# Cross attention in one fused perceiver layer: another order of the half-batches and another place for the projections

## The reference, cut to what matters

```python
x = x + cross_attention(layernorm(x), ctx_512)        # 16 batches x 64 queries, 1024 context rows of 128
x = x + self_attention(layernorm(x))
x = x + moe(layernorm(x))

# cross attention, per batch and head (16 heads):
kv_rope = kv_c * cos + rotate_half(kv_c) * sin
scores  = (q_r) @ (kv_rope @ W_kr).T                  # q_r from x, Wq, w_kc_q, W_qr
attn    = softmax(scores)                             # over the 1024 context rows
ctx_c   = attn @ kv_rope                              # 64 x 128 per head
ctx_lat = einsum('bhsd,hkd->bshk', ctx_c, w_kc_kv)
out     = ctx_lat.reshape(b, s, H * K) @ Wo.T         # 512 columns
```

## Time and profile before

| | us |
|---|---|
| median of 3 runs | 1516.76 (1516.18 to 1520.94) |
| the profiled execution | 1518.74 |
| its span, first to last instruction | 1516.9 |
| PE busy | 1361.9 (90%) |
| DVE busy | 809.9 (53%) |
| ACT busy | 734.6 (48%) |
| POOL busy | 573.7 (38%) |
| cross attention in the trace | about 155 to 802 |

### The profile page before, as it was taken

How to read it: one execution, slowest core, us unless ns; L and a number is a source line. 1 busy time by engine, 2 the same in 40 slices (tenths; PEclk the granted TensorE clock), 3 DMA queues, 4 the chain that set the end, 5 groups by cost and what they waited for, 6 DMA issues and landing times. The chain is left out here.

```text
span 1516.9 us, 22837 instructions
## 1 busy us (share of the span) xinstructions
PE 1361.9 (90%) x7136; PEld 1105.5 (73%) x7136; DVE 809.9 (53%) x1371; ACT 734.6 (48%) x1741; POOL 573.7 (38%) x346
## 2 busy tenths in 40 slices
PE   5998699999999999999985899999689979999992
PEld 4776578777777777777764688888578768777781
DVE  4434365656566666666544444444479863433235
ACT  2444465655555555555533577777521213333330
POOL 2122333333333332333103233333246466517985
PEclk9999799999999999999997999999699999999996
DMA  5786540323232323232315111112544246446667
GB/s 192 244 274 184 221 153 29 136 87 124 97 124 97 124 97 124 97 124 97 135 60 190 62 50 63 49 48 98 190 163 142 84 174 215 155 139 219 232 205 232
DMA packets 78984, 209.79 MB, mean 138 GB/s; under 512 B 5888, under 2 KB 39168, under 8 KB 72960
## 3 DMA queue, kind: packets, MB, share of 16 engines
q1 hardware_dynamic: 69472, 163.78, 30.4%
q0 software_dynamic: 7136, 38.80, 7.7%
q10 hardware_dynamic: 2304, 6.29, 1.1%
HBM read 154.59 MB, written 92.01 MB: 163 GB/s over the span
## 5 line engine op out<-in xcount | busy, mean ns | idle before, releaser
L660 DVE TENSOR_TENSOR probsT_lo<-psTr,probsT_hi 128x512 fp32r<-128x512 f32 x256 | 176.5, 690 | 199.9 <-ACT probsT_hi L610 199.5
L610 ACT CAST probsT_hi<-psTr 128x512 fp32r<-128x512 f32 x256 | 149.8, 586 | 211.7 <-PE psTr L750 211.0
L750 PE MATMUL psTr<-ident,probs 128*128 128x128 f32 x1024 | 152.5, 276 | 18.6 <-DVE probsT_lo L660 12.4
L750 PEld LDWEIGHTS psTr<-ident,probs 128*128 128x128 f32 x1024 | 122.3, 141 | 62.0 <-DVE probsT_lo L660 28.8
L527 POOL TENSOR_TENSOR ctxT_lo<-ctx_f,ctxT_hi 128x512 fp32r<-128x512 f32 x32 | 41.3, 1290 | 321.1 <-ACT ctxT_hi L579 321.1
L655 DVE TENSOR_REDUCE nmax<-psS 128x1 f32<-128x1024 f32 x128 | 155.4, 1214 | 11.5 <-PE psS L66 10.7
L572 ACT ACTIVATE probs<-psS,nmax 128x1024 f32<-128x1024 f32 x128 | 143.3, 1120 | 28.2 <-DVE nmax L655 28.2
L64 PE MATMUL bank<-w_slots,ao_first_hi 128*128 (+1 forms) x252 | 107.8, 428 | 15.3 <-DVE w_slots L1774 9.4
L64 PE MATMUL psV<-probsT_hi,kv_hi 128*128 128x512 f32 x256 | 117.3, 458 | 2.0
L64 PE MATMUL psS<-kT_hi,qe 128*128 128x512 f32 x256 | 113.1, 442 | 5.5 <-issue 4.7
L1480 POOL TENSOR_TENSOR w_slots<-w_ahead,w_slots 128x3072 fp32r<-128x3072 f32 x15 | 102.5, 6836 | 1.2
(11 more groups left out here) (268 smaller groups left out, 3328.8 us busy)
## 6 DMA issues: line engine op xcount, KB each, us to landing
w_ahead<-w_exp POOLq DMA_DIRECT2D x14, 1536.0 KB, 7.4
qe<-stage SPq DMA_DIRECT2D x16, 1024.0 KB, 6.7
qe<-qe SPq DMA_DIRECT2D x16, 1024.0 KB, 5.0
wraw<-w_pairs SPq DMA_DIRECT2D x8, 1792.0 KB, 11.3
early<-xs SPq DMA_DIRECT2D x47, 256.0 KB, 2.7
xs<-h_rows SPq DMA_DIRECT2D x47, 256.0 KB, 2.0
early<-ctx SPq DMA_DIRECT2D x16, 512.0 KB, 3.8
ao<-attn_out SPq DMA_DIRECT2D x32, 256.0 KB, 2.4
```

What stands on the lines that cost most here:

```text
L610: act.copy(PT[k % PTN].hi[:], psT[slot][:]).then_inc(turned_hi, 1)
L660: dve.tensor_tensor(out, psT[slot][:], f32(hi), ALU.subtract).then_inc(turned_free, 1)
L750: last = pe.transpose(psT[slot][:, q * P:(q + 1) * P], src(q), ident[:])
```

## The change

The four half-batches of a tile now go batch by batch inside a head half: c = 0, 1 are heads 0 to 7 of the first and second batch, c = 2, 3 heads 8 to 15. With that

- heads 0 to 3 of a tile are projected in its own c = 3, heads 4 to 7 in the next tile's c = 0, 8 to 11 in c = 1, 12 to 15 in c = 2 (`HEADS_AT`); in the last tile 4 to 15 come after c = 3. The semaphore counts halves of a projection;
- the K turns for the next tile's two batches are in c = 2 and c = 3 (steps 2 and 6), issued after the scores and ahead of the value product of the step; a second buffer holds the rotated context of the odd batch;
- the rope of the next tile's batches is on POOL's queue in c = 0 and 1; those of batches 0 and 1 are made in `build_queries`, after the second and the fourth pair's `split_low`, and the second context load is issued there;
- four K turns instead of two stand ahead of the first scores;
- residual, statistics and norm are at c = 2 (steps 4 to 7) and c = 3, k = 0; the turn of the normed rows at c = 3, k = 2;
- `kv_high` is at c = 0 and c = 3, k = 3; the probabilities' turned buffers are 3 instead of 4.

Cut to its core:

```diff
-def rope_kv(pool, keep, b):
+def rope_kv(pool, keep, b, j):
+
+    kv, kr, kt, tab = keep["kv_raw"], keep["kv_rope"][j], keep["kv_term"], keep["rope_tab"]
     ...
-        with sp.Fori(0, NP // 2 - 1) as i:
+        for p in range(2):
+            step(p, p, True)
+        sp.wait_ge(keep["rope_done"], 2)
+        sp.dma_start(keep["kv_raw"], t["ctx"][1]).then_inc(keep["kv_in"], 16)
+        with sp.Fori(1, NP // 2 - 1) as i:
     ...
-        with pool.Fori(0, NP // 2) as i:
+        pool.sem_inc(keep["rope_done"], 1)
+        for i in range(2):
             for j in range(2):
                 split_low(j, 2 * i + j)
-        pool.sem_inc(keep["rope_done"], 1)
-        pool.wait_ge(keep["tab_in"], 16)
-        rope_kv(pool, keep, 0)
+            if i == 0:
+                pool.wait_ge(keep["tab_in"], 16)
+            rope_kv(pool, keep, i, i)
+        with pool.Fori(2, NP // 2) as i:
+            for j in range(2):
+                split_low(j, 2 * i + j)
     ...
-PTN = 4
+PTN = 3
 K_STEPS, R_STEP = (2, 6), 4
+HEADS_AT = {0: {0: (4,), 1: (5,), 5: (6,), 7: (7,)}, 1: {0: (8,), 1: (9,), 5: (10,), 7: (11,)},
+            2: {0: (12,), 1: (13, 14), 3: (15,)}, 3: {5: (0,), 6: (1,), 7: (2, 3)}}
+TURN_H2_AT = (3, 2)
     ...
-        if hf == 0 and has_k and k in K_STEPS:
+        if c >= 2 and has_k and k in K_STEPS:
     ...
+        def iteration(i, first, last):
+            if not last:
+                fill(2 * i)
+                for j in range(2):
+                    load_kv(2 * i + 2 + j)
             for j in range(2):
-                load(2 * i + j, j, i, False)
-        for b in range(B, NBLK // NT):
-            sp.dma_start(t["xs_r"][b], t["zeros"]).then_inc(keep["fill_in"], 16)
+                if not last:
+                    sp.wait_ge(s_mm, RT * (HB * i + 3 + j))
+                    load_qe(2 * i + 2 + j, j)
+                if j == 0 and not first:
+                    sp.wait_ge(x1_made, i + 1)
+                    sp.dma_start(XT[:], x_d[i]).then_inc(xt_in, 16)
     ...
+                if c == 3 and not first:
+                    root(i - 1)
                 if not (first and c == 0):
                     ctx_low(n - 1, (c - 1) % HB)
-                if c == 1 and not first:
-                    root(i - 1)
-                if hf == 0 and has_k:
-                    kv_low(b + 1, 1 - j)
-                if hf == 1 and not last:
-                    pool.wait_ge(turned, place(b, 0, "K", 1, True)[0])
-                    pool.wait_ge(kv_lo, b + 2)
-                    rope_kv(pool, keep, b + 2)
-
-        iteration(0, True, False)
-        with pool.Fori(1, NT - 1) as i:
-            iteration(i, False, False)
-        iteration(NT - 1, False, True)
+                if c == 0:
+                    kv_low(2 * i + 1, 1)
+                if c == 3 and not last:
+                    kv_low(2 * i + 2, 0)
+                if c < 2 and not last:
+                    if first:
+                        pool.wait_ge(turned, 2 * c + 2)
+                    else:
+                        pool.wait_ge(turned, place(i - 1, 2 + c, "K", 1, True)[0])
+                    pool.wait_ge(kv_lo, 2 * i + c + 1)
+                    rope_kv(pool, keep, 2 * i + 2 + c, c)
     ...
-            if c == 0:
-                act.wait_ge(proj_done, i + 1)
-            act.copy(CT.hi[:, (c % 2) * H // 2:(c % 2 + 1) * H // 2, (c // 2) * S:(c // 2 + 1) * S],
+            if c % 2 == 0:
+                wait(act, proj_half, 2 * i - 1 + c // 2)
+            act.copy(CT.hi[:, (c // 2) * H // 2:(c // 2 + 1) * H // 2, (c % 2) * S:(c % 2 + 1) * S],
                      CX[:].rearrange("p (h s) -> p h s", s=S)).then_inc(ct_hi, 1)
     ...
+                    if k == 3 and c == 0:
+                        kv_high(2 * i + 1, 1)
+                    if k == 3 and c == 3 and not last:
+                        kv_high(2 * i + 2, 0)
     ...
+                    if not first and (c, k) == TURN_H2_AT:
+                        h2_high(i - 1)
     ...
-        LN_STEPS = {1: residual, 3: stats, 4: aggregate, 5: variance}
+        LN_STEPS = {(2, 4): residual, (2, 5): stats, (2, 6): aggregate, (2, 7): variance, (3, 0): norm}
     ...
+                        if k == 0 and c == 0:
+                            pe.wait_ge(turned_free, FIRST + 2 if first else place(i - 1, 3, "K", 1, True)[2])
+                            pe.wait_ge(qe_in[1], 16 * (i + 1))
+                        if k == 0 and c == 3:
+                            pe.wait_ge(turned_free, place(i, 2, "K", 1, True)[2])
+                            pe.wait_ge(qe_in[0], 16 * (i + 2))
+                        scores(n + 1, (c + 1) % 2, (c + 1) % HB // 2, k // 2)
+                    if c >= 2 and has_k and k in K_STEPS:
     ...
+                    heads = HEADS_AT[c].get(k, ()) if c == 3 or not first else ()
                     for kk in ([k - 2] if k in range(2, LT - 1) else [LT - 3, LT - 2, LT - 1] if k == LT - 1 else []):
-                        pe.wait_ge(turned_free, place(b, hf, "P", kk, has_k)[2])
+                        if kk == LT - 1:
+                            project(i if c == 3 else i - 1, heads)
+                        pe.wait_ge(turned_free, place(i, c, "P", kk, has_k)[2])
                         if kk == 0:
                             pe.wait_ge(cx_done, n + 1)
-                            pe.wait_ge(kv_lo, b + 1)
+                            pe.wait_ge(kv_lo, 2 * i + j + 1)
                         mm3(pe, psV[:], KV[j].at(ALL, kk, ALL), PT[kk % PTN].at(ALL, ALL),
                             kk == 0, kk == LT - 1).then_inc(pv_done, 1)
-                    if not first:
-                        if c == 0:
-                            project(i - 1, range(2 * k, 2 * k + 2))
-                        if (c, k) == (2, 5):
-                            turn_h2(i - 1)
-                    if last and c == 3 and k >= 2:
-                        project(i, range(max(0, k - 2) + min(k - 2, 2), k - 1 + min(k - 1, 2)))
-
-        iteration(0, True, False)
-        with pe.Fori(1, NT - 1) as i:
-            iteration(i, False, False)
-        iteration(NT - 1, False, True)
-        project(NT - 1, range(H // 2, H))
+                    if not first and (c, k) == TURN_H2_AT:
+                        turn_h2(i - 1)
+                    if k < LT - 1:
+                        project(i if c == 3 else i - 1, heads)
+
+        tiles(pe, iteration)
+        project(NT - 1, range(H // 4, H))
     ...
+            second = attn.enter_context(nc.sbuf_tensor("kv_rope_second", [P, LT * DC], F32))
+            keep["kv_rope"] = [early[:, 2], second[:]]
```

More of the change, by code:

```diff
@@ L85, with wait @@
 ALL = slice(None)
-def rope_kv(pool, keep, b):
-    kv, kr, kt, tab = keep["kv_raw"], keep["kv_rope"], keep["kv_term"], keep["rope_tab"]
+def wait(eng, sem, value):
+    if not isinstance(value, int) or value > 0:
+        eng.wait_ge(sem, value)
+def rope_kv(pool, keep, b, j):
+    kv, kr, kt, tab = keep["kv_raw"], keep["kv_rope"][j], keep["kv_term"], keep["rope_tab"]
     pair = lambda ap: ap.rearrange("p (a two) -> p a two", two=2)
@@ L417, in turn_counts @@
     at, split = {}, 0
-    for hf in range(HALVES):
-        for what in turn_order(hf, has_k):
-            at[(hf, *what)] = (len(at), split)
+    for c in range(HB):
+        for what in turn_order(c, has_k):
+            at[(c, *what)] = (len(at), split)
             split += what[0] != "R"
@@ L470, in build_cross, with place, halves, tiles @@
     AT = {True: turn_counts(True), False: turn_counts(False)}
[L472 to L482, removed]
+    def place(i, c, what, k, has_k):
+        g, m = AT[has_k][(c, what, k)]
+        return FIRST + TURNS * i + g + 1, FIRST + SPLITS * i + m + 1, FIRST + SPLITS * i + m + 1 + 2
+    def halves(i, c, last):
+        return HB * i + c, c % 2, c // 2, not last, not (last and c == HB - 1)
+    def tiles(eng, iteration):
+        iteration(0, True, False)
+        with eng.Fori(1, NT - 1) as i:
+            iteration(i, False, False)
+        iteration(NT - 1, False, True)
     block = ctx.enter_context(nc.Block())
@@ L509, in _ @@
+        tiles(sp, iteration)
+        for r in range(2 * NT - 2, NBLK // NT):
+            fill(r)
         sp.wait_ge(rope_done, B + 1)
         sp.dma_start(keep["early"][0], t["w_qkv"][0]).then_inc(keep["wqkv_in"][0], 16)
-        sp.wait_ge(turned, place(B - 2, 0, "K", 1, True)[0])
-        sp.wait_ge(kv_lo, B)
+        sp.wait_ge(turned, place(NT - 2, 2, "K", 1, True)[0])
+        sp.wait_ge(kv_lo, B - 1)
         sp.dma_start(keep["early"][1], t["w_qkv"][1]).then_inc(keep["wqkv_in"][1], 16)
@@ L593, in store_h2, with turned_k @@
             act.dma_start(h2_d[tt], H2[:]).then_inc(h2_out, 16)
-        for k in range(2):
-            act.wait_ge(turned, k + 1)
-            act.copy(KT[0].hi[:, k * BANK:(k + 1) * BANK], psT[k][:]).then_inc(turned_hi, 1)
+        def turned_k(slot, j, q, count):
+            act.wait_ge(turned, count)
```

(29 more changed lines are left out.)

141 lines of the change are left out of this document (59 added, 82 removed).

## The result

The changed kernel takes 1499.4 us (median of 7 runs, 1494.81 to 1508.97) against 1516.76 us (median of 7, 1514.5 to 1523.35). The ratio of the runs is 0.9879, with a 95% interval of 0.9849 to 0.9910. The forecast was 1500 us.

The account below looks back on a forecast made before the run. PE, busy 90%, bounds the kernel, waiting 4.6 us a tile on a chain of handovers. Terms -13.5 - 7.3 + 2.6 + 1 = -17.2 from the median 1516.76 give 1499.6, forecast 1500 us; 8 in 10 range 1492 to 1509.

Parts of the forecast that it names:

- six tiles of the loop: Cross stage's loop: spread heads cut each tile from 78.0 to 75.75 us, six times, 13.5 less.
- last tile: Last tile: no K pairs and fewer heads before the stamp, 76.35 falls to 69.05 us, 7.3 less.
- first tile: First tile: gains 4 heads in c = 3 (2.78 us), one K pair moves there from c = 0; +2.6 us.
- last `ctx_f` to the self stage: Tail: heads 4 to 7 (2.78 us) fit into the 3.1 us before the last context rows arrive; unchanged.
- start of the cross stage, query stage: Two more K turns hidden by waiting for queries, cost nothing; second context load ahead of a weight load costs 1 us.
- the replay: PE's waits per half-batch, computed from traced handover durations in the new order; loop's tile 75.75 us.
- The row with 0.55: c = 3: norm takes 0.55 us, starting before POOL's instruction; K0 waits 0.32, half-batch 20.25.
- Rival A: c = 3: norm meets POOL, takes 1.52 instead of 0.55 us; 5.3 us in all, so 1505; chance 0.15.
- B: New waits: only the moved heads and a quarter of the loop's waits come back; -10.4 us, 1507; chance 0.12.
- C: Nearly all waits go: the loop's tile falls to 74.5 us, total 1491; chance 0.06.
- E: The waits only move and the edges cancel: 1515 us; chance 0.04.
- D: POOL's rope comes late behind SP's loads: each us beyond 24 lost seven times, 1527 at 24 + 4; chance 0.03.

Follow-up runs that it names:

- run 1: Changed kernel with all 16 heads of the tile before projected in c = 0, two at each step: 1515.35 us, ratio to the kernel before 0.9973.
- run 5: Changed kernel with the four heads of c = 0 and of c = 1 at steps 3, 4, 5, 7 instead of 0, 1, 5, 7: 1496.19 us, ratio 0.9847.
- run 7: On top of run 5, DVE makes K0's low part before the reciprocal and maximum of step 2 in c = 3: 1492.9 us (one run).
- run 2: Changed kernel with the norm at c = 3, k = 1, behind the low part of P1, instead of k = 0: 1496.2 us (one run).
- Run 6: Changed kernel with ACT's cast of a batch's context at k = 2 instead of k = 3 in c = 0 and 3: 1497.12 us (one run).
- run 3: Changed kernel with the norm moved as in run 2, and ACT's context-rows cast in c = 3 one step later (k = 2): 1501.21 us (one run).
- run 4: Changed kernel, last tile only: heads 0 to 7 at steps 4 to 7 of c = 3, heads 8 to 15 behind it: 1500.41 us (one run).
- run 8: On top of run 7, the context cast at k = 2 in c = 0 and 3: 1492.15 us (median of 6), ratio to the kernel before 0.9837.

## Why the prediction was right, point by point

Measured by the same stamps, in us:

| term | predicted | measured |
|---|---|---|
| c = 0, 1, 2, 3 of the loop's tile | 18.4, 17.95, 19.15, 20.25 | 18.37, 17.85, 19.06, 20.10 |
| six tiles of the loop | -13.5 | -15.8 |
| last tile | -7.3 | -7.5 |
| first tile (first turn of probabilities to its last `ctx_f`) | +2.6 | +2.6 |
| last `ctx_f` to the self stage | 0 | +0.9, within the spread |
| start of the cross stage, query stage | +1 | +0.2, within the spread |

The mechanism was right, but the near-exact number owes something to luck. The parts forecast -17.2 us, the stamps show 19.9 less in the cross stage, and the medians of the runs differ by 17.4, with an interval of 14 to 23.

- **The bound.** That PE's waits are a chain of handovers and can be filled with heads is shown by run 1, which takes the heads back and gets 2.2 of 2.6 us a tile back, and by run 5, where c = 0 and 1 have no wait left.
- **The loop's tile.** The waits stand where the replay put them: P5 in c = 0 and c = 1, the last value product in c = 2, K0 and P4 in c = 3. Each half-batch came out up to 0.15 shorter than forecast, 0.4 together, which is the 2.3 us of the sum's difference. About half of it is the 0.05 to 0.1 that the sum charged for restarting in c = 0, 1 and 2 on top of the wait itself, and that the rows of after don't show. The rest is c = 3: there no restart was charged, but P4 turns 7.72 after P0 instead of 7.83. Its wait is 0.60 (run 7 has it at 7.12) instead of 0.70, and K0's is 0.27 (run 2 has it at 4.09, after at 4.36) instead of 0.32. Run 6 shows the cause given for c = 0 (the context cast, 0.5 us).
- **The norm.** The row with 0.55 was the right one. Runs 2 and 3 show the mechanism: 1.45 with POOL's instruction started just before, 0.54 without. The Trainium skill, SBUF — State Buffer, section "Who interferes with whom", says that the first to issue holds the shared pair and the other blocks until it is done; the trace agrees: 303.02 + 1.45 = 304.47 lies 0.28 behind the end of POOL's instruction (304.19). In the seven tiles of the kernel before and the seven of run 2 the norm ends 0.27 to 0.29 behind POOL's instruction, whether it started 0.04 or 0.16 after it, and POOL's takes its usual 1.28 to 1.29. But 0.28 is only half of the norm's own 0.54; which part of an instruction needs no port no run shows. That POOL is held by a norm that started first is not shown either, since the two overlapped by 0.06 in the loop and 0.11 at most in a last tile. Rival A is refuted for this kernel, and its price for the loop was not tried at k = 0, where it would have been paid; at k = 1 it is nothing (run 2).
- **The last tile and its tail.** 68.86 against 69.05 replayed, and heads 4 to 7 are free in the tail (run 4: 2.7 us). The 0.9 behind the last `ctx_f` is no more than scatter: the last pass of the last head starts 8.11 behind it in after and 8.08 before, and the whole way to the self stage's first cast, 18.1 in after and 17.2 before, takes 17.1 to 18.3 in runs 2 to 8, which differ from after there in nothing but run 4's four heads.
- **Rivals B, C, E** would have put the tile at 76.9, 74.5 or 78; it is at 75.4. **D**: POOL begins the first rope at 256.50, 10.6 us into the tile, without idle time before it, so the rows are there; none of PE's loads waits for a rope.
- **Query stage.** In the ten profiled executions, nine of them with the new order in this stage, the first turn of probabilities stands at 171.4 to 174.5 us, before at 174.3. A us is not to be told from that spread. PE's first K turns stand at 155.18, before at 155.40, though the weights asked for behind the context rows are issued at 66.45 instead of 64.02. The two more K turns cost at most 0.4: the first scores are at 162.47 instead of 162.06, and PE's loads still wait 3.20 before them for the queries to land, so that these hide the turns, as forecast. POOL waited 4.4 us for the second context rows and still made the next weights' low part at 78.19, where it was 77.91.

The profiled span fell by 22.5 and the cross stage by 19.9; the rest is the scatter of the later stages, which take 709.3 to 717.4 us from the self stage on in these executions though nothing in them was changed.

## What to carry to other kernels

Where the busiest engine waits a few tenths at every handover and has independent work bunched elsewhere, spread that work. Here steps shortly before the turn that waited served better than earlier ones (run 5), and a replay of one period with durations from the trace gave each half-batch to 0.15 us. Removing one link of such a chain can gain nothing (run 7) until the next link is shortened too (run 8), so look for what is late next before editing. Work that needs no late input belongs behind the loop's end if something is awaited there.

## What the runs showed of the hardware

The same tensor_scalar of 128 x 512 fp32, SBUF to SBUF, takes 0.54 us with POOL idle and 1.42 to 1.52 when a POOL tensor_tensor of 1.28 to 1.29 us has started 0.04 to 0.16 us before it. In the other order (norm first by 0.48) neither was longer than usual, 0.54 and 1.28 to 1.30. A POOL instruction that starts early in a running norm did not occur in these runs. An instruction can thus take nearly three times its time because it starts 0.04 us behind another engine's, and the loop need not notice it (run 2).
